# Edge countings at eight places, a sixth score bank in layer 1, x rows kept on chip, levels made by quarters

## The chip, the cores and the metric

The kernel runs on one core of a Trainium2 chip. The metric is the device time of one execution in microseconds (us). PE is TensorE, DVE is VectorE, ACT is ScalarE, POOL is GpSimd, SP is SyncE, whose queue issues most DMAs.

## What is computed

Two graph networks over one adjacency matrix of 8192 x 8192 int32 (about one entry in 1024 is 1), features of 64 columns. The kernel makes them three attention layers, called 0, 1 and 2:

```python
# layer 0
Wh = x @ W; We = entity_embs @ W
scores = (Wh @ a1)[:, None] + (We @ a2)[None, :]
e = where(adj > 0, leaky_relu(scores, 0.2), -9e15)
x1 = layernorm(x + elu(softmax(e, axis=1) @ entity_embs + x))
# layers 1 and 2, each a _gat_layer on h (h = x1 first)
Wh = h @ W_l
e = leaky_relu(Wh @ L1 @ a + (Wh @ L2 @ a).T + lb @ a)
h = 0.2 * x1 + 0.8 * elu(softmax(where(adj > 0, e, -9e15)) @ Wh)
# then
out = layernorm(x1 + concat(x1, h1, h2) @ mlp_w + mlp_b)
```

Softmax runs over all 8192 columns of a row, and a row of scores must be shifted by (a bound of) its maximum over the row's edges.

## The kernel before

**Tiles and blocks.** Rows go in 16 blocks (b) of 512; columns in 64 tiles (j, or t as a place in the loop) of 128. For one tile DVE (or, for some tiles of layer 0, ACT) writes the started scores of 128 columns x 512 rows into a PSUM bank (L1242 in `start_scores`), PE adds the mask into the same bank with fp8 products in two halves of the array, shape 128*64 (L813, `mask_scores`), ACT takes exp (L640, `probs`), and PE multiplies the probs with the features, two tiles at a time, also 128*64 (L854, `main`). Five banks, `eps`, are used in turn (ES = 5), so DVE can start tile j only when the probs of tile j - 5 are made (`freed`). The other three PSUM banks are `acc` (sums), `den` (denominators, made in layers 0 and 2 with shape 128*32) and `misc`. In layer 1 `den` is not used: a column of ones stands in the features.

**Counting edges.** For the bound of the maxima the kernel sorts columns into levels by their v score. `levels` makes `oneh` (128 x 64 x 32 bf16, two DVE steps over all 2048 elements, L1295 and L1297). For the next block DVE turns each quarter (m = 0 to 3) of the stored mask into `edges` (`make_edges`, L1081) at t = T_XOR[m], and PE multiplies it with `oneh` (`count_edges`, L824: 16 products of shape 128*32, four of them side by side) at t = T_HIST[m] = 35, 35, 43, 43. `edges` has two places, so the making for m waits for the counting of m - 2. Then ACT copies the counts at t = 45, PE turns them at t = 47 (L833), DVE makes the head from them at t = 51 to 53 (14 small steps, from L1099), PE turns and spreads the maxima at 56 and 57, and DVE makes `ua` at 63. So in every engine the order is written out by hand by t, and each engine runs its own list in order.

**Mask and stream.** In layer 0 SP loads the adjacency in 512 loads of 512 KB into `stage` (4 places), DVE makes bytes (L1051), SP turns them into `nt` by transposing DMAs and stores them to `nt_d`. Layers 1 and 2 load 4 MB per block from there; `stage` is then free in layer 1 and holds probs in layer 2.

**Tail.** The last block's sums are finished inside the next block: copies at t = 4 and 5, normalising at 13 and 14, features at 20 to 23, products at 27 to 31, output sums at T_Y = 35 (`tail_output`, in layer 2 followed by rstd on POOL, L562, at whose queue the adding DMAs L573 stand too). In layer 0 SP loads the block's 512 rows of x (128 KB) into `xin` for the tail (L425), although all x rows were also loaded into `feat[:, 1]` at the start for the scores. `products_out` writes the next layer's features over them, block by block.

**Between layers** nothing overlaps: the last tail, the v bounds, `levels`, counting of block 0, head. Two of the four edge makings of the next layer's block 0 stand in the last block at T_XOR[2] and T_XOR[3]; the other two come after `levels`, since `edges` has two places.

## Time and profile before

| | us |
|---|---|
| median of 3 runs | 3390.24 |
| lowest, highest | 3382.48, 3395.13 |
| the profiled execution's own time | 3391.65 |
| its span | 3389.8 |
| PE busy | 3053.4 |
| DVE busy | 2862.4 |
| ACT busy | 2282.4 |

The span runs from the first to the last instruction. Layer 0 fills it up to 1337 us, layer 1 lies between 1380 and 2285, layer 2 from 2320. Matmuls are pipelined, so their durations overlap; the distance of two starts tells what a group takes. A bracket behind a row is the engine's idle time before it and what ended it.

### The profile page before, as it was taken

The page shows a single profiled execution, that of the slowest core. Times are in us where ns is not written, and L with a number is a line of the kernel's source. Part 1 is how long each engine was busy: PE and PEld are TensorE (multiplying, and loading weights), DVE is VectorE, ACT ScalarE, POOL GpSimd, SP SyncE. Part 2 cuts the span into 40 slices and gives each one's busy share as a digit, 9 for nine tenths or more (in the row PEclk, how much of TensorE's full clock was granted, in tenths as well). Part 3 has the DMA queues.
Part 4 walks back from the last instruction along what each step waited for, and adds up shares of the span by engine and source line. Part 5 has one row for each costly group of instructions (what it writes and reads, how often), then busy time and mean ns, then how long its engine had stood idle before and what let it go on. Part 6 is the DMA issues. An engine that isn't in the chain of part 4 may idle for free. (4 is left out here: it accounts for less than half of the span.)

```text
span 3389.8 us, 53702 instructions
## 1 busy us (share of the span) xinstructions
PE 3053.4 (90%) x20369; PEld 1080.6 (32%) x20447; DVE 2862.4 (84%) x5292; ACT 2282.4 (67%) x3934; POOL 287.8 (8%) x330
## 2 busy tenths in 40 slices
PE   1599999999999998799999999997999999999998
PEld 0133333333333333233333333332333333333333
DVE  5688888888888875899999999987888888888886
ACT  0367777777777676577877777774666666666665
POOL 0000000000000000000000000001122112212211
PEclk9999999999999999899999999998999999999999
DMA  9999999999999951312121212216577767766764
GB/s 308 359 347 343 343 343 344 336 346 346 343 343 348 331 157 54 114 64 109 66 106 72 104 75 103 75 63 173 149 163 177 173 158 164 194 161 161 174 142 81
DMA packets 441749, 679.11 MB, mean 200 GB/s; under 512 B 297474, under 2 KB 318082, under 8 KB 416914
## 3 DMA queue, kind: packets, MB, share of 16 engines
q1 hardware_dynamic: 409458, 564.40, 51.3%
q0 software_dynamic: 32032, 111.27, 16.4%
q8 instruction: 161, 2.64, 0.3%
q14 instruction: 98, 0.80, 0.1%
HBM read 430.10 MB, written 77.69 MB: 150 GB/s over the span
## 5 line engine op out<-in xcount | busy, mean ns | idle before, releaser
L1242 DVE SCALAR_TENSOR_TENSOR eps<-ua,v8col,cb 128x512 f32<-128x512 f32 x2800 | 1960.5, 753 | 243.4 <-ACT prob L640 180.1
L640 ACT ACTIVATE prob<-eps,v2col 128x512 f32<-128x512 f32 x2564 | 1641.2, 688 | 635.6 <-PE eps L813 622.6
L854 PE MATMUL acc<-prob,feat 128*64 128x512 f32 x5128 | 1333.7, 599 | 6.3 <-ACT acc_s L645 6.3
L813 PE MATMUL eps<-nt,nbig 128*64 128x512 fp8e4 (+1 forms) x5444 | 1022.5, 386 | 150.6 <-DVE eps L1242 142.8
L813 PEld LDWEIGHTS eps<-nt,nbig 128*64 128x64 bf16 (+1 forms) x5444 | 327.4, 109 | 1115.0 <-DVE eps L1242 726.5
L1051 DVE TENSOR_SCALAR mi<-stage 128x1024 uint8<-128x1024 int32 x512 | 353.5, 692 | 132.7 <-DMA stage<-in_adj_dram 131.5
L854 PEld LDWEIGHTS acc<-prob,feat 128*64 128x64 f32 x5128 | 338.1, 136 | 256.0 <-issue 94.2
L640 ACT ACTIVATE stage<-eps,v2col 128x512 f32<-128x512 f32 x336 | 214.3, 686 | 95.6 <-PE eps L813 93.9
L863 PE MATMUL den<-prob,ones 128*32 128x512 f32 x2048 | 246.4, 599 | 0.0
L1081 DVE TENSOR_SCALAR edges<-nt 128x2048 int32<-128x2048 int32 x192 | 234.1, 1219 | 7.1 <-PE misc L824 7.0
L824 PE MATMUL misc<-edges,oneh 128*32 128x512 fp8e4 x3072 | 190.9, 391 | 52.7 <-DVE edges L1081 37.9
L619 ACT ACTIVATE eps<-ub,v8col 128x512 f32<-128x512 f32 x272 | 189.1, 695 | 0.0
L854 PE MATMUL acc<-stage,feat 128*64 128x512 f32 x672 | 174.2, 597 | 0.0
L640 ACT ACTIVATE mi<-eps,v2col 128x512 f32<-128x512 f32 x172 | 110.7, 686 | 47.3 <-PE eps L813 46.5
L824 PEld LDWEIGHTS misc<-edges,oneh 128*32 128x32 bf16 x3072 | 79.9, 98 | 188.2 <-issue 76.1
L573 POOL DMA_DIRECT2D prob<-prob x96 | 83.7, 886 | 426.8 <-PE acc L854 404.4
L556 POOL DMA_DIRECT2D u_d<-urow x32 | 17.6, 551 | 1105.7 <-ACT urow L686 1105.7
L863 PEld LDWEIGHTS den<-prob,ones 128*32 128x32 f32 x2048 | 53.4, 109 | 181.9 <-issue 181.9
L552 POOL TENSOR_TENSOR rstd<-mom,half 128x4 f32<-128x4 f32 x16 | 23.1, 1444 | 1031.4 <-DVE mom L1137 1031.4
L877 PE MATMUL den<-prob,ones 128*32 128x512 f32 x648 | 100.6, 602 | 8.8 <-DMA prob<-prob 4.6
L810 PE MATMUL eps<-mrow,onesb 128*64 128x512 bf16 (+1 forms) x453 | 94.1, 386 | 2.4 <-issue 2.4
L854 PE MATMUL acc<-mi,feat 128*64 128x512 f32 x344 | 89.5, 600 | 0.0
(174 smaller groups left out, 1686.8 us busy)
## 6 DMA issues: line engine op xcount, KB each, us to landing
stage<-in_adj_dram SPq DMA_DIRECT2D x512, 512.0 KB, 6.4
nt<-nt_d SPq DMA_DIRECT2D x128, 1024.0 KB, 6.1
nt_d<-nt SPq DMA_DIRECT2D x64, 1024.0 KB, 7.1
prob<-prob POOLq DMA_DIRECT2D x96, 512.0 KB, 5.8
stage<-stage POOLq DMA_DIRECT2D x64, 512.0 KB, 6.4
mi<-mi POOLq DMA_DIRECT2D x32, 512.0 KB, 6.5
ub<-u_d SPq DMA_DIRECT2D x48, 256.0 KB, 5.3
xy_d<-xin POOLq DMA_DIRECT2D x32, 256.0 KB, 3.2
```

Of the source, the lines that this page charges most:

```text
L573: nc.gpsimd.dma_start(buf[:, o:o + 2, :], buf[:, o + 2:o + 4, :], accum_op=ALU.add).then_inc(added(b, g, h)[0], 16)
L619: nc.scalar.activation(eps[:, j % ES, :], ub[:, par, :], ACT.Relu, bias=v8col[:, j:j + 1], scale=1.0 - ALPHA).then_inc(s_filla, 1)
L640: nc.scalar.activation(weights(l, b, j), eps[:, j % ES, :], ACT.Exp, bias=v2col[:, j:j + 1]).then_inc(s_p, 1)
L810: nc.tensor.matmul(et[c:c + cols, :], onesb[:, c:c + cols], mrow[:, par, :], start=False, stop=False, skip_group_check=True, tile_position ...
L813: mm = nc.tensor.matmul(et[c:c + cols, :], nbig[:, c:c + cols], edge, start=False, stop=True, skip_group_check=True, tile_position=(0, c))
L824: mm = nc.tensor.matmul(misc[s * HB:(s + 1) * HB, :], oneh[:, m * MT + j, :], half_block(edges[:, n % 2, :], m, j), start=(m == 0 and k == 0),
L854: mm = nc.tensor.matmul(acc[h:h + C, :], feat[:, l % 2, j, 0:C], weights(l, b, j), start=(k == 0), stop=(k == NT // 2 - 1))
L863: mm = nc.tensor.matmul(den[32 * i:32 * i + 32, :], ones[:, 0:32], weights(l, b, QUAD * k + i), start=(k == 0), stop=(k == NT // QUAD - 1))
L877: mm = nc.tensor.matmul(den[32 * i:32 * i + 32, :], ones[:, 0:32], weights(2, b, DEN * g + j), start=(g == DEN_ORDER[0] and n == 0), stop= ...
L1051: dv.tensor_scalar(out, src, 0, ONE8, ALU.is_le, ALU.mult).then_inc(s_mask, 1)
L1081: dv.tensor_scalar(edges[:, n % 2, :].bitcast(I32), nt[:, b % 2, m, :].bitcast(I32), EDGE_FLIP, None, ALU.bitwise_xor).then_inc(s_xor, 1)
L1242: dv.scalar_tensor_tensor(eps[:, j % ES, :], ua[:, par, :], v8col[:, j:j + 1], cb[:, par, :], ALU.add, ALU.max).then_inc(s_fill, 1)
```

## The change

- `T_XOR` and `T_HIST` move, and each counting is made in two parts of 8 products, at t = T_HIST[m] and the next t: 33, 34, 36, 37, 40, 41, 43, 44.
- Layer 1 uses `den` as a sixth score bank (`BANKS`, `bank`, `freed`).
- The tail of layer 0 reads x from `feat[:, 1]` (`x_rows`); the loads of x rows go, `tail_output` waits for the stored x1 rows of the block before, and the column of ones for layer 1 is set when layer 0 is over.
- `levels` makes `oneh` in quarters with a semaphore step for each, and PE counts quarter by quarter; the column scalings have a semaphore of their own.
- All four edge makings for the next layer's block 0 stand in the last block; quarters 2 and 3 go into `stage` (`edge_place`).

```diff
-T_XOR = (29, 32, 40, 41)
-T_HIST = (35, 35, 43, 43)
+T_XOR = (29, 32, 39, 42)
+T_HIST = (33, 36, 40, 43)
+BANKS = (ES, ES + 1, ES)
...
+        def edge_place(l, b, m):
+            if l > 0 and b == 0 and m >= 2:
+                return spare[:, m - 2, :]
+            return edges[:, m % 2, :]
...
+        def bank(l, j):
+            n = j % BANKS[l]
+            return den[:, :] if n == ES else eps[:, n, :]
         def freed(l, b, j):
-            if j >= ES:
-                return tile(l, b, j) - ES + 1
-            last = max(i for i in range(NT) if i % ES == j)
+            if j >= BANKS[l]:
+                return tile(l, b, j) - BANKS[l] + 1
+            k = l if b else l - 1
+            last = max(i for i in range(NT) if i % BANKS[k] == j % BANKS[k])
             return tile(l, b, last) - NT + 1
...
-                    if tail:
+                    if tail and l > 0:
                         xin_free(l, b - 1)
                         xin_load(l, b - 1)
...
-            def count_edges(l, b, m):
+            def count_edges(l, b, m, parts=(0, 1)):
                 n = MV * blk(l, b) + m
                 pe.wait_ge(s_xor, n + 1)
-                for k in range(MT // 4):
+                for k in [k for k in range(MT // 4) if k // (MT // 8) in parts]:
...
-                mm.then_inc(s_hist, 1)
+                if 1 in parts:
+                    mm.then_inc(s_hist, 1)
...
-                pe.wait_ge(s_oneh, l + 1)
                 for m in range(MV):
+                    pe.wait_ge(s_oneh, l * MV + m + 1)
                     count_edges(l, 0, m)
...
                         for m in range(MV if head else 0):
-                            if t == T_HIST[m]:
-                                count_edges(l, b + 1, m)
+                            for part in range(2):
+                                if t == T_HIST[m] + part:
+                                    count_edges(l, b + 1, m, (part,))
...
+                if l > 0 and b == 0 and m >= 2:
+                    dve.wait_ge(s_mask, NU)
+                elif n >= 2:
                     dve.wait_ge(s_hist, n - 1)
...
+            def x_rows(b):
+                return feat[:, 1, b * RT:(b + 1) * RT, 0:C]
...
                 if l == 0:
                     dve.wait_ge(s_h, blk(l, b) + 1)
+                    if b > 0:
+                        dve.wait_ge(s_x1, 16 * b)
...
                     dve.wait_ge(s_p, freed(l, b, j))
+                    if (l, b, j) == (1, 0, ES):
+                        dve.wait_ge(s_dene, NB)
...
-                step(dv.tensor_tensor(oneh[:, :, :], over(kk[:, :], "p (t o) -> p t o"),
-                                      over(iota[:, :], "p (o k) -> p o k"), ALU.is_equal), s_startseq, at + 11)
-                step(dv.tensor_tensor(oneh[:, :, :], oneh[:, :, :], over(ww[:, :].bitcast(F32), "p (t o) -> p t o"),
-                                      ALU.mult), s_startseq, at + 12)
+                for m in range(MV):
+                    q = slice(m * MT, (m + 1) * MT)
+                    dv.tensor_tensor(oneh[:, q, :], over(kk[:, q], "p (t o) -> p t o"),
+                                     over(iota[:, :], "p (o k) -> p o k"), ALU.is_equal).then_inc(s_startseq, 1)
+                    dve.wait_ge(s_startseq, at + 11 + m)
+                    dv.tensor_tensor(oneh[:, q, :], oneh[:, q, :], over(ww[:, q].bitcast(F32), "p (t o) -> p t o"),
+                                     ALU.mult).then_inc(s_oneh, 1)
                 dv.tensor_scalar(v8col[:, :], v, 1.0 - ALPHA, None, ALU.mult)
-                step(dv.tensor_scalar(v2col[:, :], v, ALPHA, None, ALU.mult), s_oneh, l + 1)
+                dv.tensor_scalar(v2col[:, :], v, ALPHA, None, ALU.mult).then_inc(s_cols, 1)
+                dve.wait_ge(s_cols, l + 1)
...
+                    if l == 1:
+                        dv.memset(feat[:, 1, :, C - 1:C], 1.0).then_inc(s_one, 1)
                     bounds(l)
                     levels(l)
-                    for m in range(2, MV):
-                        make_edges(l, 0, m)
...
                         if not head_ and l < NLAYER - 1:
-                            for m in range(2):
-                                if t == T_XOR[m + 2]:
+                            for m in range(MV):
+                                if t == T_XOR[m]:
                                     make_edges(l + 1, 0, m)
```

## Rows read from the trace of the kernel before

**Rows 1.** The page: the span, then the busy time of each engine.

```profile
span 3389.8 us, 53702 instructions
...
PE 3053.4 (90%) x20369; PEld 1080.6 (32%) x20447; DVE 2862.4 (84%) x5292; ACT 2282.4 (67%) x3934; POOL 287.8 (8%) x330
```

**Rows 2.** Windows: busy time per engine, PE clock, DMA share, GB/s.

```profile
895.00:970.00 75.00, 72.14 (x505) 25.37 (x504) 65.24 (x124) 54.31 (x96) 3.31 (x3) 1.00 1.09 346
...
1273.00:1337.00 64.00, 63.87 (x424) 22.53 (x418) 37.43 (x68) 49.66 (x89) 2.81 (x3) 1.00 0.15 60
1337.00:1380.00 43.00, 16.49 (x126) 8.91 (x125) 20.36 (x64) 5.32 (x14) 2.38 (x3) 0.61 0.33 122
...
1667.98:1724.82 56.84, 53.24 (x341) 19.11 (x340) 53.96 (x96) 44.09 (x79) 1.28 (x2) 1.00 0.24 89
...
2519.09:2585.59 66.50, 62.97 (x430) 21.92 (x427) 56.47 (x108) 43.80 (x75) 13.04 (x14) 1.00 0.70 169
```

**Rows 3.** Waits in layer 1: total us, times, longest.

```profile
DVE eps L1242 <- ACT prob L640: 36.3, 50, 1.7
```

**Rows 4.** Timeline of PE in one block of layer 1: start, duration.

```profile
1693.37 1.03 PE L854 MATMUL acc<-prob,feat 128*64 128x512 f32 x4
1694.33 1.91 PE L824 MATMUL misc<-edges,oneh 128*32 128x512 fp8e4 x32
1696.17 0.62 PE L813 MATMUL eps<-nt,nbig 128*64 128x512 fp8e4 x4
1696.62 1.02 PE L854 MATMUL acc<-prob,feat 128*64 128x512 f32 x4
1697.48 0.60 PE L813 MATMUL eps<-nt,nbig 128*64 128x512 fp8e4 x4
1697.91 1.02 PE L854 MATMUL acc<-prob,feat 128*64 128x512 f32 x4
...
1700.87 0.41 PE L813 MATMUL eps<-nt,nbig 128*64 128x512 fp8e4 x2 [0.26 <-DVE eps L1242]
...
1706.61 1.08 PE L833 MATMUL misc<-fold,hs 128*128 128x32 f32 x8
```

**Rows 5.** Timeline of DVE in the same block of layer 1.

```profile
1705.13 0.76 DVE L1242 SCALAR_TENSOR_TENSOR eps<-ua,v8col,cb 128x512 f32<-128x512 f32 x1 [1.01 <-ACT prob L640]
...
1707.72 0.29 DVE L1099 TENSOR_SCALAR he<-misc 128x128 int32<-128x128 int32 x1
...
1718.55 1.42 DVE L1242 SCALAR_TENSOR_TENSOR eps<-ua,v8col,cb 128x512 f32<-128x512 f32 x2 [0.88 <-ACT prob L640]
```

**Rows 6.** Timeline of PE in a block of layer 0.

```profile
1236.79 1.92 PE L863 MATMUL den<-prob,ones 128*32 128x512 f32 x16
1238.53 1.91 PE L824 MATMUL misc<-edges,oneh 128*32 128x512 fp8e4 x32
1240.37 0.41 PE L813 MATMUL eps<-nt,nbig 128*64 128x512 fp8e4 x2
```

**Rows 7.** Chain that ended last, in one block of layer 2: start, us, what.

```profile
2550.04 12.91 DMA prob<-prob
```

**Rows 8.** Timeline of PE in the same block of layer 2.

```profile
2560.65 1.02 PE L854 MATMUL acc<-stage,feat 128*64 128x512 f32 x4
2563.08 1.07 PE L877 MATMUL den<-prob,ones 128*32 128x512 f32 x8 [1.41 <-DMA prob<-prob]
```

**Rows 9.** Timeline of all engines between layers 1 and 2.

```profile
2300.86 2.29 DVE L1295 TENSOR_TENSOR oneh<-kk,iota 128x2048 bf16<-128x2048 int32 x1
...
2305.90 4.37 PE L824 MATMUL misc<-edges,oneh 128*32 128x512 fp8e4 x48 [7.37 <-DVE oneh L1297]
...
2307.94 2.54 DVE L1081 TENSOR_SCALAR edges<-nt 128x2048 int32<-128x2048 int32 x2 [2.15 <-PE misc L824]
...
2311.64 0.60 ACT L690 ACTIVATE hs<-misc 128x512 f32<-128x512 f32 x1 [15.29 <-PE misc L824]
```

**Rows 10.** Waits in the last block of layer 1.

```profile
DVE eps L1242 <- ACT prob L640: 1.1, 2, 0.7
```

**Rows 11.** DMA queues in 8 us of layer 0 that hold one x load: packets, MB, share.

```profile
q1 hardware_dynamic: 528, 0.13, 7.2%
```

More of the change, by code:

```diff
@@ L68 @@
 SEQ_SETUP = 4
-SEQ_START = 12
+SEQ_START = 14
 SEQ_HEAD = 12
@@ L248, in build @@
         s_oneh = sem("levels_on_columns")
+        s_cols = sem("score_columns_made")
         s_hist = sem("edges_counted")
@@ L310, in half_block @@
             return v[:, g, o, :].bitcast(FP8)
+        spare = stage[:, :, :].rearrange("p s w -> p (s w)").bitcast(U8).rearrange("p (e w) -> p e w", w=MT * BI)
+        def edge_place(l, b, m):
+            if l > 0 and b == 0 and m >= 2:
+                return spare[:, m - 2, :]
+            return edges[:, m % 2, :]
         def landed(l, b, m):
@@ L423, in xin_load @@
             def xin_load(l, b):
-                if l == 0:
-                    sp.dma_start(xin[:, :, 0:C], x_v[b]).then_inc(s_xin, 16)
-                else:
-                    sp.dma_start(xin[:, :, :], xy_v[l - 1, b]).then_inc(s_xin, 16)
+                sp.dma_start(xin[:, :, :], xy_v[l - 1, b]).then_inc(s_xin, 16)
             def xin_free(l, b):
-                if b == 0 and l != 1:
+                if b == 0 and l == 2:
                     return
@@ L517, in _ @@
                 blocks(body)
-                xin_free(l, NB - 1)
-                xin_load(l, NB - 1)
+                if l > 0:
+                    xin_free(l, NB - 1)
+                    xin_load(l, NB - 1)
             for i in range(2 * MV):
@@ L618, in start_scores @@
                     act.wait_ge(s_ub[par], ub_count(l, b, par))
-                nc.scalar.activation(eps[:, j % ES, :], ub[:, par, :], ACT.Relu, bias=v8col[:, j:j + 1],
+                nc.scalar.activation(bank(l, j), ub[:, par, :], ACT.Relu, bias=v8col[:, j:j + 1],
                                      scale=1.0 - ALPHA).then_inc(s_filla, 1)
@@ L639, in probs @@
                 act.wait_ge(s_z, tile(l, b, j) + 1)
-                nc.scalar.activation(weights(l, b, j), eps[:, j % ES, :], ACT.Exp,
+                nc.scalar.activation(weights(l, b, j), bank(l, j), ACT.Exp,
                                      bias=v2col[:, j:j + 1]).then_inc(s_p, 1)
@@ L666, in products_out @@
                         if l == 0:
-                            if b == 0 and i == 0:
-                                act.wait_ge(s_one, 1)
                             nc.scalar.activation(feat[:, d, bass.ds(b * RT + 2 * i, 2), 0:C - 1],
@@ L803, in mask_scores @@
                 on_act = j in ON_ACT[l]
-                et = eps[:, j % ES, :]
+                et = bank(l, j)
                 m, o = divmod(j, MT)
@@ L824, in count_edges @@
                         mm = nc.tensor.matmul(misc[s * HB:(s + 1) * HB, :], oneh[:, m * MT + j, :],
-                                              half_block(edges[:, n % 2, :], m, j), start=(m == 0 and k == 0),
+                                              half_block(edge_place(l, b, m), m, j), start=(m == 0 and k == 0),
                                               stop=(m == MV - 1 and k == MT // 4 - 1), skip_group_check=True,
                                               tile_position=(0, s * HB))
-                mm.then_inc(s_hist, 1)
+                if 1 in parts:
+                    mm.then_inc(s_hist, 1)
             def turn_counts(l, b):
@@ L990, in body @@
                             pe.wait_ge(s_cbe, blk(l, 0) + 1)
+                            if l == 1:
+                                pe.wait_ge(s_one, 1)
                             column_sums(l)
@@ L1078, in make_edges @@
                 dve.wait_ge(s, count)
-                if n >= 2:
+                if l > 0 and b == 0 and m >= 2:
+                    dve.wait_ge(s_mask, NU)
+                elif n >= 2:
                     dve.wait_ge(s_hist, n - 1)
-                dv.tensor_scalar(edges[:, n % 2, :].bitcast(I32), nt[:, b % 2, m, :].bitcast(I32), EDGE_FLIP, None,
+                dv.tensor_scalar(edge_place(l, b, m).bitcast(I32), nt[:, b % 2, m, :].bitcast(I32), EDGE_FLIP, None,
                                  ALU.bitwise_xor).then_inc(s_xor, 1)
@@ L1156, in tail_elu @@
                 step(dv.tensor_tensor(z[:, :, :], g[:, :, 0:C], spread(rden[:, :]), ALU.mult), seq, at + 3)
-                dve.wait_ge(s_xin, 16 * (blk(l, b) + 1))
                 if l == 0:
-                    step(dv.tensor_tensor(z[:, :, :], z[:, :, :], xin[:, :, 0:C], ALU.add), seq, at + 4)
+                    step(dv.tensor_tensor(z[:, :, :], z[:, :, :], x_rows(b), ALU.add), seq, at + 4)
+                else:
+                    dve.wait_ge(s_xin, 16 * (blk(l, b) - NB + 1))
                 if not (l == 0 and b == 0):
@@ L1171, in tail_features @@
                 if l == 0:
-                    step(dv.tensor_tensor(hn[:, :, :], hn[:, :, :], xin[:, :, 0:C], ALU.add), seq, at + 2)
+                    step(dv.tensor_tensor(hn[:, :, :], hn[:, :, :], x_rows(b), ALU.add), seq, at + 2)
                     row_sums_to_means(hn[:, :, :], seq, at + 2)
@@ L1239, in start_scores @@
                     dve.wait_ge(s_p, freed(l, b, j))
+                    if (l, b, j) == (1, 0, ES):
+                        dve.wait_ge(s_dene, NB)
                 elif j == 0:
                     dve.wait_ge(s_prime, 1)
-                dv.scalar_tensor_tensor(eps[:, j % ES, :], ua[:, par, :], v8col[:, j:j + 1], cb[:, par, :],
+                dv.scalar_tensor_tensor(bank(l, j), ua[:, par, :], v8col[:, j:j + 1], cb[:, par, :],
                                         ALU.add, ALU.max).then_inc(s_fill, 1)
@@ L1326, in _ @@
                     node_sums(1)
-                    dv.memset(feat[:, 1, :, C - 1:C], 1.0).then_inc(s_one, 1)
                     masks(20, 24)
```

4 lines of the change are left out of this document (2 added, 2 removed).

## The prediction

> **What bounds the kernel now.** I read the page first, then windows by stage, then waits and timelines inside one block of each layer. The page has PE at 90% of a span of 3389.8 us and DVE at 84% [rows 1]; the profiled execution took 3391.65 us, 1.9 us outside its span and 1.4 us above the median of 3390.24.
>
> The windows tell the layers apart [rows 2]. A block of layer 0 takes 75.0 us with PE busy 72.1 and DMA at a share of 1.09: PE and the adjacency stream bind nearly together. A block of layer 1 takes 56.84 us, PE busy 53.2. Its DVE waits for banks only 36.3 us in the whole layer, 2.4 us for each of the 15 blocks in that window [rows 3], so it too is nearly full. A block of layer 2 takes 66.5 us with PE busy 63.0. Between layers the work is serial: 43 us in which PE is busy 16.5 at a mean clock of 0.61.
>
> So PE time added in a block is rarely free. The question of this change is whether bank waits of DVE are worth more than switches of PE's tile shape.
>
> **Countings in halves.** Before, 64 counting products of a block stand at two places, 32 each. Eight places of 8 do the same products. The price is what PE loses at each place. In layer 1 [rows 4] a pair of mask products is followed by main at 0.43 us and main by masks at 0.86. Around the count, main to count is 0.96, the 32 products take 1.84, and masks to main 0.45. Eight rounds of four products at the pace of a mask pair (0.43 us for two rounds) are 1.71 us. Loss per place: 0.10 + 0.13 + 0.02 = 0.25 to 0.27 us; I use 0.26. Two places become eight: 6 x 0.26 = 1.6 us more per block in layers 1 and 2.
>
> In layer 0 it is worse, since both old places (t = 35 and 43) stand right behind the denominators, which have the same 128*32 shape: from their start to the mask behind the count is 3.58 us [rows 6], two times 1.71 and 0.16, one place's loss for both. Of the new places only t = 43 stands behind them. So seven new switches: 7 x 0.26 = 1.8 us per block. The even places (34, 36, 40, 44) stand between two mask products; the trace has no such place. Bounds per switch: 0, if the shapes follow each other there as masks follow main, and 0.52, if both sides pay as around a whole place; I take 0.26, the row it is nearest to.
>
> The Trainium skill, "TensorEngine Tiling (Array Packing)", section Key Properties, says that a change of the tiling mode, not of the tile alone, drains the array. That speaks against this change, and by it every new place pays; these rows agree with 0.26 us for the two switches of a place.
>
> **Where that lands, layer 1.** From t = 33 to the turned counts at t = 47 PE is a chain with one gap worth naming, 0.26 us [rows 4]. DVE is stopped twice. The first time, 1.01 us before 1705.13 [rows 5], looks as if the long count caused it and six banks or short counts would cure it. But the head of the next block needs the turned counts, which PE starts at 1706.61 and ends at about 1707.6, and DVE starts it at 1707.72: DVE earlier at tile 49 would only wait there. PE's arrival at t = 47 decides, and it moves by 1.6 less the 0.3 of its own wait, which spread edge makings (39 and 42 for 40 and 41) remove: +1.3 us. DVE works 14 small steps from there while PE runs dry, so the delay goes on. The second stop, 0.88 us before 1718.55 [rows 5], is a real bank wait and the sixth bank lifts it; yet 64 tiles over 6 banks leave 4, so the first four tiles of the next block again follow their bank's last prob at four tiles. ACT gives those one after another; between 0 and 0.88 us is left of the gain, and I take 0.5. Net +0.8 us per block, 15 blocks: **+12 us**. Bounds: -2.4 (all of DVE's waits) to +1.6, -36 to +24.
>
> **Layer 2** keeps five banks. Its chain goes from the output step at t = 35 through rstd and the adding DMA, 12.91 us [rows 7], to the den at 2563.08, where PE had waited 1.41 us [rows 8]. PE now comes 1.6 us later: it uses up that wait and is 0.1 to 0.2 late. 15 x 0.1: **+1.5 us**. The cover is the DMA; without it 24 us. A gain is left out, since nothing that the change shortens is in this chain.
>
> **Layer 0.** 1.8 us more of PE against 2.9 us of idle PE in the block of 75.0 [rows 2]. In layer 1, which waits for no stream, 3.6 us of idle PE remain, so such idle is mostly not to be had; I let half of it, 1.4, absorb: +0.4 us, 14 blocks: **+5.6 us**. x rows on chip remove a load of 128 KB per block. One such load in 8 quiet us took 7.2% of 16 engines, 0.58 us [rows 11]; where the stream ends the wait that is a gain of 0.58 x 15 = 8.7 us, where PE ends it nothing. I take nothing and keep it for the low bound; high bound 14 x 1.8 = 25. SP no longer issues that load; it queued in front of adjacency loads, which wait for DVE. The added wait for the last stored x1 block at t = 35 concerns a store of 64 tiles earlier: it is met when DVE comes there, and so is the wait for layer 0's last denominators at tile 5 of layer 1. The ones column moves into the layer change: 0.1 us.
>
> **Levels by quarters, edges made earlier.** Between layers 1 and 2 [rows 9] the levels start at 2300.86, PE counts from 2305.90, two edge makings (2.54 us) interrupt it, and the counts are copied at 2311.64. After: a step over all levels takes 2.29 us, so one over a quarter takes 0.57 and a fixed part, which I take as 0.1; two of them about 1.35. The first counting can start at 2302.3. Four countings of 16 products take 0.9 us each at full clock, 1.7 at half (twice 0.85); DVE's quarters end at 2306.3, so the copy comes between 2307.3 and 2309.2. PE had stood idle for 7.37 us before the old counting, and such a stretch has a mean clock of 0.61 [rows 2], so I take one and a half countings at half clock: 2308.2. Gain 3.4 us (2.5 to 4.2), twice: **-6.8 us**. The two column scalings leave the path with it.
>
> All four edge makings now stand in the last block of the layer before: two more, 2.5 us. In layer 0 DVE is busy 37 of 64 us there [rows 2]: free. In layer 1 DVE waits only 1.1 us in all of that block [rows 10], so 2.4 - 1.1: **+1.3 us**. If its cover were gone, 2.5.
>
> **Sum.** 5.6 + 12 + 1.5 - 6.8 + 1.3 + 0.1 = +13.7 us on 3391.65 is 3405.3; less 1.4 to the median: **3404 us**. A measurement tells about 0.5% from no change, 17 us; my forecast lies inside, near the edge.
>
> **Rivals.**
> *Bank waits were the price (faster).* Short countings let ACT and DVE go on, the sixth bank takes DVE's 36 us of waits, the stream gives 8, the layer changes 5.4. 3390 - 49 = 3341; with half of the first, 3359. For it: DVE is nearly full in layer 1 and waits just after the counts. Against it: the turned counts come from PE, which had no time to spare. It decides if the switch at even places costs nothing: then PE gains back 4 x 0.26 of the 1.6. Chance 0.28.
> *Every switch is paid in full (slower).* Nothing absorbs the new switches: 25 + 24 + 24 - 5.3 = +68, 3458; with half of it 3425. For it: PE has 95% in the windows. Its place is t = 33 to 47; its point is PE later at t = 47 than the DMA of layer 2 by over 0.2 us, which a switch above 0.3 us gives. Against it: PE has measured waits there. Chance 0.20.
> *Only the layer changes move.* Switches and the sixth bank cancel in each block, the x load is hidden: 3390 - 5 = 3385. Chance 0.10.
>
> **How the numbers follow.** Forecast (3388 to 3420) 0.42, of it 0.30 within 0.5% and 0.12 above. The fast rival gives 0.26 faster and 0.02 same, the slow one 0.20 slower, the last 0.08 same and 0.02 faster. Faster 0.28, same 0.40, slower 0.32. Range 3350 to 3430: it leaves out the ends of both rivals, some 0.09 each.
>
> **What would show it.** Count places of 8 products with about 0.26 us lost each, at even places too; PE's start of the turned counts in layer 1 later by about 1.3 us against the start of its block; period of layer 1 near 57.6 (rival: 54.5 to 55.5), of layer 2 near 66.5, PE's wait for the DMA at the den gone; of layer 0 near 75.4; the layer changes shorter by 3 to 4 us; DVE's 0.88 us wait gone and a wait for the turned counts in its place. If layer 1 comes out under 56 us, my chain through t = 47 is wrong.

## The result

The changed kernel takes 3396.78 us (median of 20 runs, 3393.74 to 3400.43) where the kernel before takes 3389.91 (20 runs, 3382.48 to 3400.92): a ratio of 1.002, with a 95% interval of 1.0014 to 1.0027. That is 6.9 us slower, half of the 13.7 that the prediction summed up, and within the 0.5% that it called no change. The two profiled executions lie nearer to each other, 3391.65 and 3393.74 us: the first is 1.7 us above its median, the second is the lowest of its 20 runs, 3.0 below. So the stages below add up to a difference of 2 us and not of 7.

The page of the changed kernel: the span, the busy time of each engine, and the chain of work that ended last.

```profile
span 3392.0 us, 53779 instructions
...
PE 3112.6 (92%) x20447; PEld 1040.8 (31%) x20447; DVE 2869.3 (85%) x5310; ACT 2303.6 (68%) x3934; POOL 289.2 (9%) x330
...
PE 22%; DVE 7%; ACT 1%; DMA 1%; issue 1%; POOL 0%; POOLq 0%; ACTq 0%; DVEq 0%
```

The same line of the kernel before:

```profile
PE 14%; DVE 10%; DMA 5%; ACT 1%; issue 1%; POOL 1%; POOLq 0%; another core or an unknown queue 0%; ACTq 0%; DVEq 0%
```

PE is busy 59 us more than in [rows 1]. Some 10 of them are records missing from that trace (x20369 for 20447 products): the second profile of the kernel before (run 15) has them all and shows 3063.9 us, 49 less than here. PE's share of the chain grew from 14 to 22%, and that of the DMA fell from 5 to 1%. By stage (a block of layer 0, of layer 1, the two layer changes from the copy of the last sums to the copy of the new counts, a block of layer 2), to be laid beside [rows 2]:

```profile
895.00:970.00 75.00, 73.58 (x508) 24.19 (x504) 65.16 (x124) 54.67 (x96) 3.31 (x3) 1.00 1.10 345
1661.90:1719.29 57.39, 54.29 (x342) 18.31 (x340) 53.97 (x96) 44.47 (x78) 1.29 (x2) 1.00 0.24 88
1333.01:1362.40 29.39, 13.64 (x112) 7.39 (x109) 14.32 (x53) 3.55 (x12) 2.38 (x3) 0.65 0.24 84
2285.42:2308.32 22.90, 10.95 (x88) 6.04 (x88) 11.90 (x39) 2.89 (x10) 1.28 (x2) 0.63 0.29 99
2519.09:2585.59 66.50, 64.47 (x433) 21.26 (x431) 56.68 (x107) 44.36 (x73) 13.16 (x14) 1.00 0.70 169
```

ACT copies each block's sums once (`acc_s<-acc`), so the distance of two copies is the period of a block. In us, between the two profiled executions:

| stretch | before | after | change | predicted |
|---|---|---|---|---|
| start, to the first copy | 213.1 | 214.9 | +1.9 | 0 |
| layer 0, 14 blocks | 1060.5 | 1053.7 | -6.7 | +5.6 |
| last block of layer 0 | 63.8 | 64.4 | +0.5 | 0 |
| change 0 to 1 with the block behind it | 103.0 | 99.3 | -3.7 | -2.6 |
| layer 1, 14 blocks | 56.85 each | 57.42 each | +8.0 | +11.2 |
| last block of layer 1 | 48.2 | 49.2 | +1.0 | +1.3 |
| change 1 to 2 with the block behind it | 102.3 | 99.4 | -2.9 | -3.3 |
| layer 2, 14 blocks | 66.08 each | 66.38 each | +4.2 | +1.4 |

These are PE's rows in a block of layer 1 of the changed kernel. What counts is the distance of two starts: 1.01 us from main to a count here (0.96 at the later places), 0.54 or 0.55 for eight products up to the mask pair behind them, and 0.34 from a mask pair to a count (0.31 at the least in this block).

```profile
1685.96 1.08 PE L865 MATMUL acc<-prob,feat 128*64 128x512 f32 x4
1686.97 0.61 PE L834 MATMUL misc<-edges,oneh 128*32 128x512 fp8e4 x8
1687.51 0.41 PE L823 MATMUL eps<-nt,nbig 128*64 128x512 fp8e4 x2
1687.85 0.61 PE L834 MATMUL misc<-edges,oneh 128*32 128x512 fp8e4 x8
1688.40 0.41 PE L823 MATMUL den<-nt,nbig 128*64 128x512 fp8e4 x2
1688.64 1.02 PE L865 MATMUL acc<-prob,feat 128*64 128x512 f32 x4
...
1697.96 0.41 PE L823 MATMUL eps<-nt,nbig 128*64 128x512 fp8e4 x2
1698.30 0.61 PE L834 MATMUL misc<-edges,oneh 128*32 128x512 fp8e4 x8
1698.85 0.41 PE L823 MATMUL eps<-nt,nbig 128*64 128x512 fp8e4 x2
...
1701.33 0.85 PE L844 MATMUL misc<-fold,hs 128*128 128x32 f32 x6
```

A mask pair with another behind it takes 0.22; in front of a count it is 0.34, and eight products take 0.55 where two rounds at full pace take 0.43: 0.12 and 0.12. So an even place, too, costs about 0.24 us. DVE in the same block waits for the turned counts (line 1115) and less for banks:

```profile
1699.19 0.76 DVE L1266 SCALAR_TENSOR_TENSOR eps<-ua,v8col,cb 128x512 f32<-128x512 f32 x1 [0.46 <-ACT prob L652]
1700.26 0.76 DVE L1266 SCALAR_TENSOR_TENSOR eps<-ua,v8col,cb 128x512 f32<-128x512 f32 x1 [0.31 <-ACT prob L652]
1702.44 0.29 DVE L1115 TENSOR_SCALAR he<-misc 128x128 int32<-128x128 int32 x1 [1.43 <-PE misc L844]
...
1713.27 0.76 DVE L1266 SCALAR_TENSOR_TENSOR eps<-ua,v8col,cb 128x512 f32<-128x512 f32 x1 [0.22 <-ACT prob L652]
...
1715.08 1.42 DVE L1266 SCALAR_TENSOR_TENSOR eps<-ua,v8col,cb 128x512 f32<-128x512 f32 x2 [0.45 <-ACT prob L652]
```

Against [rows 5], the stop of 1.01 us before tile 49 has become two of 0.46 and 0.31, and in front of the turned counts there are now 1.43. The 0.88 behind the head has become 0.22 and 0.45, so only 0.21 of it is gone.

### The profile page after: what moved, and what is told of

Same layout as the page of the kernel before. It is cut to its first block and busy times, and to the rows that moved or that the text cites. A ratio compares the mean times of both kernels' runs of the same rounds, so it can differ in the third digit from the quotient of the medians.

```text
span 3392.0 us, 53779 instructions
## 1 busy us (share of the span) xinstructions
PE 3112.6 (92%) x20447; PEld 1040.8 (31%) x20447; DVE 2869.3 (85%) x5310; ACT 2303.6 (68%) x3934; POOL 289.2 (9%) x330
## 5 line engine op out<-in xcount | busy, mean ns | idle before, releaser
L1266 DVE SCALAR_TENSOR_TENSOR eps<-ua,v8col,cb 128x512 f32<-128x512 f32 x2640 | 1868.8, 753 | 259.9 <-ACT prob L652 194.9
L652 ACT ACTIVATE prob<-eps,v2col 128x512 f32<-128x512 f32 x2404 | 1562.2, 689 | 625.2 <-PE eps L823 606.9
L823 PE MATMUL eps<-nt,nbig 128*64 128x512 fp8e4 (+1 forms) x5157 | 1001.5, 388 | 105.7 <-DVE eps L1266 104.2
L823 PEld LDWEIGHTS eps<-nt,nbig 128*64 128x64 bf16 (+1 forms) x5157 | 308.3, 109 | 1033.6 <-DVE eps L1266 635.8
L834 PE MATMUL misc<-edges,oneh 128*32 128x512 fp8e4 x3008 | 235.9, 394 | 44.3 <-DVE edges L1097 36.6
L874 PE MATMUL den<-prob,ones 128*32 128x512 f32 x2048 | 246.3, 598 | 0.0
L834 PEld LDWEIGHTS misc<-edges,oneh 128*32 128x32 bf16 x3008 | 49.6, 96 | 259.7 <-issue 221.5
L1266 DVE SCALAR_TENSOR_TENSOR den<-ua,v8col,cb 128x512 f32<-128x512 f32 x160 | 120.4, 753 | 0.5
L652 ACT ACTIVATE prob<-den,v2col 128x512 f32<-128x512 f32 x160 | 110.3, 690 | 8.8 <-PE den L823 4.8
L820 PE MATMUL eps<-mrow,onesb 128*64 128x512 bf16 (+1 forms) x483 | 105.6, 386 | 0.0
```

The costliest lines, as they stand in the source:

```text
L652: nc.scalar.activation(weights(l, b, j), bank(l, j), ACT.Exp, bias=v2col[:, j:j + 1]).then_inc(s_p, 1)
L820: nc.tensor.matmul(et[c:c + cols, :], onesb[:, c:c + cols], mrow[:, par, :], start=False, stop=False, skip_group_check=True, tile_position ...
L823: mm = nc.tensor.matmul(et[c:c + cols, :], nbig[:, c:c + cols], edge, start=False, stop=True, skip_group_check=True, tile_position=(0, c))
L834: mm = nc.tensor.matmul(misc[s * HB:(s + 1) * HB, :], oneh[:, m * MT + j, :], half_block(edge_place(l, b, m), m, j), start=(m == 0 and k = ...
L874: mm = nc.tensor.matmul(den[32 * i:32 * i + 32, :], ones[:, 0:32], weights(l, b, QUAD * k + i), start=(k == 0), stop=(k == NT // QUAD - 1))
L1266: dv.scalar_tensor_tensor(bank(l, j), ua[:, par, :], v8col[:, j:j + 1], cb[:, par, :], ALU.add, ALU.max).then_inc(s_fill, 1)
```

## The experiments

Each run had the kernel before beside it on its chip; the ratios are against that. The kernel before took 3388.1 to 3390.9 us from chip to chip, so medians of runs on different chips are told apart to some 3 us only. "Fold" below is the time from a block's copy of its sums to the start of the turned counts (t = 47), in the third block of layer 1, and "rest" is what follows up to the next copy. "Quiet" blocks of layer 0 are those that the adjacency stream does not lengthen; most kernels repeat theirs to 0.02 us. Diffs leave out lines at "...".

**1. The changed kernel with whole countings at the old places.** This undoes the first item of the change alone.

```diff
-T_XOR = (29, 32, 39, 42); T_HIST = (33, 36, 40, 43)   # in two parts
+T_XOR = (29, 32, 40, 41); T_HIST = (35, 35, 43, 43)   # whole
```

> The changed kernel with the countings whole again at 35, 35, 43, 43 and the edge makings at 29, 32, 40, 41; all else as changed. Theory S (each change of PE's tile shape costs 0.24 us and delays the turned counts): block of layer 1 from 57.40 back to 56.6, below the 56.84 of before by what the sixth bank gives; layer 2 from 66.4 to 66.1; layer 0 about 75.0; in all 3397 - 12 - 4 = about 3381 us. Rival B (the sixth bank or the new waits cost the time, not the switches): layer 1 stays at 57.4, total 3393 to 3397. Rival D (layer 0 gained through short counts): layer 0 goes back to 75.7 on average, total 7 us more than theory S says.

3376.08 us, ratio 0.9966 (0.9954 to 0.9979): some 20 us faster than the changed kernel (18 by the ratios) and faster than the kernel before. Layer 1 takes 56.61 (fold 38.65, rest 17.96), as expected. Quiet blocks of layer 0 took 73.96, where about 75.0 had been expected, and the total came out 5 us under the expected one. So all that makes the change slower is in the halves and the edge makings moved for them, and what stays of it is a gain of 12 us.

**2. Whole countings at the old places, edge makings spread as in the change.**

```diff
-T_HIST = (33, 36, 40, 43)   # in two parts
+T_HIST = (35, 35, 43, 43)   # whole; T_XOR stays (29, 32, 39, 42)
```

> The changed kernel with the countings whole at 35, 35, 43, 43, but the edge makings left at 29, 32, 39, 42. Theory S, with its second half (PE's own waits at t = 42 and 43, 0.6 us in layer 1 and 1.5 us in layer 0, come from two edge makings in a row on DVE): layer 1 at 56.0 per block, layer 0 down to 73.5, or to 74.4 if the adjacency stream ends the waits there, layer 2 at 66.1; total about 3363 us. Rival: DVE has to wait at t = 39 for the count of quarter 0, which now ends after t = 35 only, and hands the gain back: layer 1 at 56.6 to 56.8, total as with the old edge makings, 3380.

3379.24 us, 0.9972 (0.9961 to 0.9984); layer 1 56.61. The 56.0 of the text did not come and neither did the 3363, so my reason for PE's own wait before tile 43 (two makings in a row) fell. The rival's numbers came, 56.6 and 3380, but in layer 1 not by its mechanism: DVE waits for no count there. PE's wait is where it was; PE in that block:

```profile
1685.13 0.38 PE L823 MATMUL eps<-nt,nbig 128*64 128x512 fp8e4 x2
1685.95 0.41 PE L823 MATMUL eps<-nt,nbig 128*64 128x512 fp8e4 x2 [0.43 <-DVE eps L1265]
...
1687.15 1.91 PE L834 MATMUL misc<-edges,oneh 128*32 128x512 fp8e4 x32
```

The distance 0.82 against 0.22 of two mask pairs makes the stop 0.60 us. DVE has no idle time in the 9 us before it, in this run and in run 1, so its whole work up to tile 43 decides it, wherever the makings stand. In the kernel before it was the same 0.60, in two parts. The rows that lie between those of [rows 4]:

```profile
1699.20 1.02 PE L854 MATMUL acc<-prob,feat 128*64 128x512 f32 x4
1700.21 0.41 PE L813 MATMUL eps<-nt,nbig 128*64 128x512 fp8e4 x2
```

Main to masks is 1.01 for 0.86 elsewhere, and from there to the mask pair at 1700.87 [rows 4] it is 0.66 for 0.22: 0.15 and 0.45. The bracket told only 0.26 of it.

In layer 0 the rival's mechanism did come. Quiet blocks took 74.50 us against the 73.96 of run 1, and DVE's making at t = 39 now waits for the counting at t = 35. The waits between 213 and 1275 us (us in all, times, longest), of run 1 and of this one:

```profile
DVE edges L1096 <- PE misc L834: 2.2, 1, 2.2
```

```profile
DVE edges L1096 <- PE misc L834: 18.2, 14, 2.2
```

That is 1.2 us in each of 13 blocks. Runs 8, 9 and 10, which keep a making at 39, have it too (14 to 18 us in all); what it costs there no run shows.

**3. The changed kernel with x loads again** (`xin_load` in layer 0's tail, the tail reads `xin`; the wait for stored x1 rows stays).

```diff
+                if l == 0:
+                    sp.dma_start(xin[:, :, 0:C], x_v[b]).then_inc(s_xin, 16)
...
```

> The changed kernel with the loads of x rows of layer 0 back (128 KB per block, tail reads them from xin). Theory S: PE sets the pace of layer 0, its blocks stay at 75.03 us, total 3397 +- 2. Rival X (the load made the irregular blocks of 76.9 to 78.7 us in layer 0): they come back, layer 0 is 5 to 9 us longer, total about 3404, and its runs scatter more.

3400.02 us, 1.0033 (1.0021 to 1.0045): 3.2 us more than the changed kernel by the medians, 4.4 by the ratios, whose intervals overlap, so the size is not settled. Quiet blocks of layer 0 stay at 75.03, and more blocks are long (seven above 75.5 us where the changed kernel has three).

**4. The changed kernel with five banks in layer 1.**

```diff
-BANKS = (ES, ES + 1, ES)
+BANKS = (ES, ES, ES)
```

> The changed kernel with five banks in layer 1 as well. Theory S: the turned counts come at the same time in the block, but DVE's bank wait behind the spread maxima is back: layer 1 at 57.6, total 3.5 us above the changed kernel, about 3400. Rival B (the sixth bank costs): layer 1 falls below 57.4, total below 3397. Rival M (bank waits are the price of a block): layer 1 at 58.5 or more, total 3413.

3401.51 us, 1.0039 (1.0026 to 1.0051), as expected. Layer 1 57.64: fold 39.43 as with six, rest 18.21 against 17.96. The sixth bank gives 0.25 us per block, all of it behind the head.

**5. The kernel before with only the halves.**

```diff
-T_XOR = (29, 32, 40, 41); T_HIST = (35, 35, 43, 43)   # whole
+T_XOR = (29, 32, 39, 42); T_HIST = (33, 36, 40, 43)   # in two parts; last blocks' makings stay at 40, 41
```

> The kernel before with its countings in halves at the eight new places and the edge makings at 29, 32, 39, 42; five banks, x loads, levels as before. Theory (the halves alone carry the loss; each place costs 0.24 to 0.26 us of PE in layer 1): layer 1 about 57.5 to 57.65 us per block against 56.84, layer 2 about 66.4, layer 0's quiet blocks about 75.0 to 75.1, layer changes as before (33.7 and 27.1 us from copy to copy); total about 3404 to 3409 against 3389. Rival (the sixth bank or the dropped x load had a share in the loss, and the halves cost less alone): layer 1 at or under 57.1, total under 3397.

3409.93 us, 1.0064 (1.0052 to 1.0077). Layer 1 57.66 (fold 39.44, rest 18.21), layer 2 66.37, quiet blocks of layer 0 75.03. The total is 1 us above the expected band, the periods are in it. The halves alone cost 22 us.

**6. The kernel before with only the x rows on chip.**

```diff
-                    step(dv.tensor_tensor(z[:, :, :], z[:, :, :], xin[:, :, 0:C], ALU.add), seq, at + 4)
+                    step(dv.tensor_tensor(z[:, :, :], z[:, :, :], x_rows(b), ALU.add), seq, at + 4)
...
```

The added wait for stored x1 rows and the moved column of ones come with it.

> The kernel before with one edit: the tail of layer 0 takes its rows of x from the features on chip, and no x rows are loaded. If the x load takes a place before adjacency loads in the queue and so makes some blocks of layer 0 long (77 to 79 us where the quiet ones take 75.0), those go: the 13 blocks of layer 0 that take 986.2 us now come to 977 to 980, total 3383 to 3387, and the runs scatter less. If it is hidden, as the prediction took it: 986, total 3388 to 3391. Layers 1 and 2 the same in both.

3378.9 us (11 runs), 0.9976 (0.9967 to 0.9985): 8 to 9 us from 128 KB less per block (5 to 11 by the interval). That is 4 us below the expected band. Layer 0's 13 blocks take 975.5 instead of 986.2 (981.4 in run 15), layer 1 the same 56.87. DVE's waits between 213 and 1275 us (us in all, times, longest), first of the kernel before, then of this one:

```profile
DVE eps L1242 <- ACT prob L640: 72.9, 92, 3.4
DVE mi L1051 <- DMA stage<-in_adj_dram: 64.1, 56, 4.0
```

```profile
DVE eps L1246 <- ACT prob L638: 81.9, 102, 3.4
DVE mi L1049 <- DMA stage<-in_adj_dram: 47.6, 46, 4.2
```

The wait for the adjacency falls by 16.5 us, and 9 of them come back as waits for banks. (In the second profile of the kernel before, run 15, the two are 77.0 and 58.6, so the shift may be no more than 11 and 5.)

**7 to 9. Where whole countings stand.** Three versions of the changed kernel, with whole countings at four, three and two places.

```diff
+T_HIST = (33, 37, 41, 43)                          # 7
+T_HIST = (35, 35, 41, 43)                          # 8
+T_HIST = (35, 35, 41, 41); T_XOR = (29, 32, 39, 41) # 9
```

> The changed kernel with whole countings of 16 products at 33, 37, 41 and 43: four places where it has eight, and where the one with whole countings at 35, 35, 43, 43 has two. Theory (each place is a drain of PE of about 0.24 us, but up to tile 43 DVE sets the pace, so only what PE must do from there to the turned counts moves the block): layer 1 at or just under 56.6 us per block (about 56.4), layer 0's quiet blocks 74.4 to 74.7, total 3378 to 3384. Rival (each added place is paid in full wherever it stands): layer 1 at 56.6 + 2 x 0.13 = 56.9 or more by half the step from two to eight places, total 3386 or more.

3366.64 us, 0.994 (0.9926 to 0.9954); layer 1 56.47 (fold 38.50), quiet blocks of layer 0 74.10. Layer 1 is as expected, but the total is 11 us under the expected band.

> The changed kernel with whole countings at 35, 35, 41 and 43 and edge makings at 29, 32, 39, 42: against whole countings at 35, 35, 43, 43 it takes 16 products from behind tile 43 to before it. Theory (after tile 43 PE alone stands before the turned counts, up to it DVE's work does): 0.86 us less PE work behind tile 43 and one place more, so layer 1 at 56.2 (56.6 less 0.4), layer 2 unchanged at 66.4, layer 0's quiet blocks 74.5 to 74.8; total about 3374 to 3377. Rival (PE's whole work from 33 to 47 decides, wherever a place stands): layer 1 at 56.6 + 0.13 or more, total 3381 or more.

3356.77 us, 0.991 (0.9897 to 0.9924); layer 1 56.22 (fold 38.26), as expected, but layer 0's quiet blocks took 73.63, where 74.5 to 74.8 had been expected, layer 2 66.02 for 66.4, and the total is 17 us under the band.

> The changed kernel with whole countings at 35, 35, 41, 41 and edge makings at 29, 32, 39, 41: two places of 32 products, the second one before PE's stop at tiles 42 and 43 instead of behind it. The theory as the last runs leave it: in layer 1 the fold starts 38.03 us into the block with two places and no stop of PE, 0.24 us later per further place, and 0.60 us later if nothing stands in that stop; with six banks 17.96 us follow. So the fold at 38.0 and a block of 56.0 us, against 56.22 with places at 35, 41, 43 and 56.60 with 35, 43. Rival (up to tile 43 DVE's own work sets the pace, so a place before it is free): the same fold as with three places, 38.25, and 56.2 us. Layer 2 at 66.0 to 66.1 in both. Total by the theory 3350 to 3355, by the rival 3355 to 3359.

3355.06 us, 0.9893 (0.988 to 0.9907); layer 1 56.00, fold 38.03: the theory's fold, and a total where its band and the rival's meet. PE in run 9, with no stop from the first count to the fold:

```profile
1667.85 1.91 PE L834 MATMUL misc<-edges,oneh 128*32 128x512 fp8e4 x32
...
1672.30 0.38 PE L823 MATMUL eps<-nt,nbig 128*64 128x512 fp8e4 x2
1672.51 0.38 PE L823 MATMUL den<-nt,nbig 128*64 128x512 fp8e4 x2
1672.73 1.02 PE L865 MATMUL acc<-prob,feat 128*64 128x512 f32 x4
1673.68 1.91 PE L834 MATMUL misc<-edges,oneh 128*32 128x512 fp8e4 x32
1675.53 0.62 PE L823 MATMUL eps<-nt,nbig 128*64 128x512 fp8e4 x4
...
1679.52 1.08 PE L844 MATMUL misc<-fold,hs 128*128 128x32 f32 x8
```

Together with runs 1 and 5 they give one law. The expectation of run 7 had said that up to tile 43 DVE sets the pace and places there are free; that is wrong, although its number, 56.4, is nearly right. From run 8 to run 7 one place more costs 0.24, as everywhere. Each place costs, and once the stop of 0.60 is filled with counting work, no other stop is left to fill:

| kernel | places | stop open | fold | by the law |
|---|---|---|---|---|
| before, run 1 | 2 | yes | 38.63, 38.65 | 38.63 |
| run 9 | 2 | no | 38.03 | 38.03 |
| runs 8 and 10 | 3 | no | 38.26 | 38.27 |
| run 7 | 4 | no | 38.50 | 38.51 |
| changed kernel, run 5 | 8 | no | 39.43, 39.44 | 39.47 |

The law is 38.03, plus 0.24 for each place above two, plus 0.60 if the stop is open; then 18.21 follow with five banks and 17.96 with six. Layer 0 obeys it as well, if a place right behind the denominators is counted as free: 73.63 us with one paid place (runs 8 and 9), 74.10 with three (run 7), 75.03 with seven (changed kernel, run 5), 0.23 per place. That was the prediction's own reading of [rows 6]. It does not hold the wait of run 2, whose quiet blocks take 0.54 us more than run 1's with the same places.

**10. The kernel before with the third counting at 41** and the edge makings at 39 and 42 that go with it.

```diff
-T_XOR = (29, 32, 40, 41); T_HIST = (35, 35, 43, 43)
+T_XOR = (29, 32, 39, 42); T_HIST = (35, 35, 41, 43)
```

> The kernel before with one thing moved: countings at 35, 35, 41, 43 and edge makings at 29, 32, 39, 42; five banks, x loads and levels as before. Theory: in layer 1 the fold at 38.27 instead of 38.63 us into the block and a block of 56.5 us (38.27 + 18.21) against 56.84; layer 2 at 66.0 to 66.1; layer changes as before; layer 0 bound by the adjacency stream as long as the x loads are in it, so its quiet blocks stay at 75.0 and its 13 blocks at 980 to 986. Total 3377 to 3384 against 3388. Rival (layer 0 hangs on PE and DVE around t = 43 and not on the stream): quiet blocks under 74.5, its 13 blocks at 970 to 976, total 3368 to 3376.

3374.82 us, 0.9953 (0.994 to 0.9965). Layer 1 56.47 (fold 38.26), as expected. Layer 0's 13 blocks took 972.2 us and the total lies in the rival's band, both the rival's numbers: moving 16 products by two tiles gives layer 0 more (9 to 14 us) than layer 1 (5), with the x loads still in it. So layer 0 was not bound by the stream alone. The 13 blocks of run 8, which has no x loads, took 966.5.

**11. Of the change only the levels by quarters and the early edge makings.**

```diff
 # the changed kernel, with
+BANKS = (ES, ES, ES); T_XOR = (29, 32, 40, 41); T_HIST = (35, 35, 43, 43)   # whole, and x loads
...
```

The wait for stored x1 rows and the place of the column of ones stay as changed.

> Of the change only the levels by quarters and the four early edge makings; countings, banks and x loads as before. Theory (the two layer changes give 4.2 us each from copy to copy, the last block of layer 1 takes 1.0 back, nothing else moves): layer 0's 13 blocks at 983 to 987, layer 1 at 56.85 us per block, layer 2 at 66.1, total 3380 to 3382 against 3388. Rival (part of what the layer change gives is paid back by PE in the first block behind it, which then waits for features or bounds): total 3384 or more.

3391.05 us, 1.0003 (0.9994 to 1.0012). This missed: no gain at all, though the layer changes are 3.1 and 3.0 us shorter from copy to copy, and with their first blocks 2.8 and 3.7. In its trace the start (+1.3), the last block of layer 1 (+1.0), layer 0 (+2.1) and layer 2 (+1.9) take it back.

**12 and 13. What the levels are worth on the kernel of run 9.** That kernel with whole levels in layer 0 only; and with levels and edge makings as in the kernel before.

```diff
+                whole = l == 0     # 12;  whole = True in 13
+                for m in range(1 if whole else MV):
+                    q = slice(0, NT) if whole else slice(m * MT, (m + 1) * MT)
...
```

> The kernel with countings at 35, 35, 41, 41, with the levels of layer 0 made in two whole steps as before and those of layers 1 and 2 in quarters. Theory (the quarters cost at the start of layer 0, where the adjacency stream waits for DVE behind them): the stretch from the start of the levels to the next mask made goes from 5.6 back to 5.0 us, and the first block's sums are copied 1.3 to 1.6 us earlier than with quarters, at 213.5 to 214.1 us instead of 215.4; layers 1 and 2 and their changes the same. Rival (the later start is the stream's own scatter, or its cause is elsewhere): the copy stays at 214.8 to 215.5. Total 3353 to 3357 by the theory, too near to the version with quarters to be told from it by medians.

3349.53 us, 0.9887 (0.9873 to 0.99), the lowest median of all, though its ratio is not told apart from run 9's 0.9893. The total is below the expected band, and the reason given fails: the first copy comes at 215.5 us, as the rival had it, although the stretch behind the levels is back at 4.9 us.

> The kernel with countings at 35, 35, 41, 41, with the levels and the edge makings of the layer changes as in the kernel before. Theory (the layer changes are worth what the traces show): the changes from copy to copy 33.7 and 27.1 us again instead of 29.5 and 23.2, the last block of layer 1 at 48.2 instead of 49.2, the start 1.4 us earlier: 8.3 - 1.0 - 1.4, 5.9 us slower than 3355, so 3359 to 3363, a ratio of 0.9905 to 0.992. Rival (the gain is paid back later in blocks, as the run with the levels alone looks): 3353 to 3357, a ratio of 0.9885 to 0.990, with the layer changes just as long as in the theory.

3355.26 us, 0.9907 (0.9893 to 0.992), on the same chip 5.7 us behind run 12, with no overlap of the two (3353.1 to 3360.35; 3348.42 to 3351.6). Layer changes 33.5 and 27.3 us against 29.6 and 23.4; with the first blocks 7.7 us, less 1.5 for the last block of layer 1: 6.2. The start takes 1.4 of that back, and layers 0 and 2, which scatter, add 0.8. So the part is worth about 6 us there. Its ratio is the theory's; the 3355 in itself lies in the rival's band, but on this chip the kernel before was 2.5 us faster than beside run 9.

**14. Run 11 without the added wait of `tail_output` for stored x1 rows.**

```diff
-                    if b > 0:
-                        dve.wait_ge(s_x1, 16 * b)
```

> The levels and early edge makings alone, as before, and without the wait of layer 0's output step for the stored x1 rows of the block before. If that wait costs, layer 0's 13 blocks come from 986.9 to 981 or less and the total to 3384 or less; if it is met when DVE comes there, as the prediction took it, the total stays at 3388 to 3392.

3385.25 us (12 runs), 0.9989 (0.998 to 0.9999); layer 0 982.9. This lies between the two expectations, and its interval touches that of run 11, so it settles nothing. Neither trace shows DVE waiting at that step.

**15. The kernel before, profiled again.**

> The kernel before, profiled a second time. If the blocks of layer 0 that wait for the adjacency stream scatter, the 13 blocks that took 986.2 us come out at another sum, by 3 us or more, with other blocks long, while layer 1 takes 56.84 per block again and the layer changes 33.7 and 27.1; if each kernel has its own pattern, they come out at 986 with the same blocks long.

3388.76 us, 1.0002 (0.9992 to 1.0011). Layer 0's 13 blocks took 981.4 us instead of 986.2, with other blocks long; layer 1 56.87; the changes 33.8 and 27.9. Layer 2 took 66.15 per block instead of 66.08. So a single trace tells a period of layer 1 to 0.03 us, a sum over layer 2 to 1 us at best and a sum over layer 0 to 5 us only. The trace shown before the prediction caught a long layer 0, and that of the changed kernel a run 3 us below its median. So the -6.7 of layer 0 in the table is too large: if all of both deviations lay there, it would be -2.

## Why the prediction was right and wrong

**The verdict held and the sum was twice the truth**, with errors of both signs in it, so that it held is in part luck. By parts of the change: the halves were to cost 5.6 + 19.5 + 1.5 = 26.6 us and cost 22 (run 5); the sixth bank was to give 7.5 and gave about 3.7, 0.25 per block (run 4). These two errors nearly cancel. What is left of the sum's excess, some 6 us, fits the x rows, which were put at nothing. Taken in the order of its steps:

**Price of a place: right.** 0.26 was foretold from the whole places of [rows 4], 0.24 was measured, at even places too, and in layer 0 with its seven paid places. The Trainium skill, TensorEngine Tiling (Array Packing), Key Properties, says that a change of the tiling mode drains the array. The rows agree: a place pays at both of its sides, 0.12 each, whether 8, 16 or 32 products stand between.

**Layer 1: mechanism right, sizes off.** Predicted 1.6 - 0.3 - 0.5 = +0.8 per block; measured 1.44 - 0.60 - 0.25 = +0.59, and 0.57 in the table. The sixth bank was taken at 0.5; of the 0.88 us that it was to lift, 0.67 is still there, in two waits. PE's wait was read from a bracket, and the distances of starts in the very same rows give 0.60. The reason for it going was wrong too: counting work at 40 and 41 fills it, the spread makings do not (run 2).

**Layer 2: mis-sized.** +1.5 became +4.2, or 3.1 against the second profile of the kernel before. PE's wait of 1.41 for the DMA was to absorb nearly all. It is gone: PE waited 13.4 us for DMAs at the denominators of layer 2 before, in 13 waits, and 0.6 after. Its waits between 2420 and 3360 us, of the kernel before and of the changed one:

```profile
PE den L877 <- DMA stage<-stage: 4.9, 5, 1.6
PE den L877 <- DMA prob<-prob: 4.6, 4, 1.4
PE den L877 <- DMA mi<-mi: 3.9, 4, 1.4
```

```profile
PE den L888 <- DMA stage<-stage: 0.4, 1, 0.4
PE den L888 <- DMA mi<-mi: 0.2, 1, 0.2
```

The cover is 13.4 / 14 = 0.96 us per block in the mean, not the 1.4 of one block. Of 1.44 us more it would leave 0.5; 0.30 was measured (0.22 against the second profile). The blocks are bound by PE now, nine of the 14 at 66.30 or 66.31 us. A mean over the layer, not one row, was the number to take.

**Layer 0: the step that failed.** "Where the stream ends the wait that is a gain of 8.7 us, where PE ends it nothing. I take nothing." Run 6 measured 8 to 9 on the kernel before, the very number that was put aside, and run 3 measured 3 to 5 on the changed one. With the 8.7 taken, the forecast of layer 0 would have been -3.1, where the traces show -6.7, or -2 if all of their distance from the medians lay there. The rest of that part held as far as two traces tell, which is 5 us: the halves were to cost 5.6 us, and against the kernel with x rows alone the changed one takes 6.1 more in its 14 blocks. That the load costs less with eight places is likely and not shown, since the two intervals overlap. It fits a cover that both parts share: with eight places PE sets the quiet block at 75.03 with the load or without it, with two most blocks are at 75.0 or above with the load, and they come down to 74.0 without it (runs 1 and 6). The window's 72.1 of 75.0 us PE busy [rows 2] said that PE was not the only bound, and DVE's 64 us of waits for the adjacency, which the rows do not show, would have said what else was.

**Layer changes: right, and better than thought.** From copy to copy 4.3 and 4.2 us less, where 3.4 was foretold (2.5 to 4.2). The quarters came as estimated (0.69 a step, 1.33 from one quarter to the next, for 1.35). What was off was the clock behind them. The change from layer 1 to 2 in the changed kernel, by windows:

```profile
2297.00:2303.00 6.00, 0.95 (x3) 0.57 (x3) 4.10 (x19) 0.25 (x1) 1.28 (x2) 0.50 0.24 72
2303.00:2305.00 2.00, 1.72 (x20) 0.73 (x24) 1.97 (x4) 0.00 (x0) 0.00 (x0) 0.50 0.96 232
2305.00:2306.30 1.30, 1.30 (x20) 0.61 (x16) 1.27 (x3) 0.00 (x0) 0.00 (x0) 0.64 0.95 384
2306.30:2308.30 2.00, 1.97 (x36) 0.68 (x28) 1.04 (x4) 0.00 (x0) 0.00 (x0) 1.00 1.03 430
```

Counting starts at 2303.28 with a granted clock of 0.50, the 1.2 GHz level, and the last quarters run at 1.00, 2.4 GHz: PE has become busy while DVE still makes levels, so the slow stretch is hidden behind DVE. In the kernel before the counting too began at 0.50 (2305.90 to 2307.94) and ended at 1.00 (2310.20 to 2311.64), but it all stood behind the levels. In the changed kernel's timeline, the two steps of the first quarter, the first counting, the weights of the last, and the copy:

```profile
2301.77 0.69 DVE L1321 TENSOR_TENSOR oneh<-kk,iota 128x512 bf16<-128x512 int32 x1
2302.49 0.69 DVE L1324 TENSOR_TENSOR oneh<-oneh,ww 128x512 bf16<-128x512 bf16 x1
...
2303.28 3.20 PE L834 MATMUL misc<-edges,oneh 128*32 128x512 fp8e4 x32 [3.85 <-DVE oneh L1321]
...
2307.22 0.55 PEld L834 LDWEIGHTS misc<-stage,oneh 128*32 128x32 bf16 x16 [0.37 <-DVE oneh L1324]
2308.32 0.60 ACT L700 ACTIVATE hs<-misc 128x512 f32<-128x512 f32 x1 [11.07 <-PE misc L834]
```

The copy follows 1.1 us behind the last quarter, not the 1.9 of the forecast. Of the gain, 0.6 and 1.3 us go again in the first blocks behind the changes, which have eight places themselves.

**Not foreseen:** the start is 1 to 2 us longer in most kernels that have this part (first copy at 213.3 to 215.5 us, in the others at 212.6 to 214.1). The levels there take 0.7 us longer, but whole levels did not bring it back (run 12). And the last block of layer 0 takes 0.5 us more with a making at 42 (64.35) and none with the last one at 41 (63.84, run 9); I had called it free.

**Rivals.** The fast one said that short countings free ACT and DVE: DVE's waits for banks in layer 1 did fall, from 36.3 [rows 3] to 22.0 us, but waits for the turned counts, 21.4 us in all, took their place, as foretold. The slow one asked for every place to be paid in full: in layer 1 places are, and 0.85 of 1.44 is given back by the filled stop and the sixth bank.

**Open:** why the levels alone show none of their 6 us in run 11 and 4 in run 14, and where the start's 1 to 2 us come from. Layer 0's scatter is as large as either.

## What to carry to other kernels

Before cutting a piece of PE work into more places, count the places: here each cost 0.24 us wherever PE had no stop, and cutting lost 22 us where moving half of the late work ahead of the one stop, whole, won 16 (runs 5 and 10). Read a stop from the distance of two starts against the same pair elsewhere, and its worth from the sum over the layer; a bracket showed less than half of it and one block half too much. Where two resources bind nearly together, price a removed transfer by the waits for the stream, and expect that its worth may shrink as the other resource fills.

## What the runs showed of the hardware

Eight products of 128*32 between mask pairs of 128*64 cost 0.24 us beyond their own pace, about what sixteen (runs 7 and 8) or thirty-two (0.25 [rows 4]) cost; a count right behind the denominators, which have its own shape, loses 0.16 together with them [rows 6]. A load of 128 KB per block of 75 us, 7.2% of the DMA engines for 8 us [rows 11], took about 0.6 us of each block of layer 0 (run 6; 0.3 to 0.7 by the interval), all that its share is worth. And PE's granted clock, 0.50 in a stretch with 0.95 us of PE work in 6, rose to 1.00 while the counting ran. So PE work between the layers was cheaper here when it started early, behind DVE's levels, than behind them in one piece.
